# Gate input moved from VectorE to TensorE and ScalarE, and the Newton step of LayerNorm from GpSimd to VectorE

## What is computed

```python
xn = _layernorm(x)                       # (x - mean) / sqrt(var + 1e-5)
s  = scan_forward(xn) + scan_backward(xn)
h  = gelu(xn @ w1[sel] + b1[sel])
g  = silu(xn + 0.3 * ((h @ w2[sel] + b2[sel]) @ Wo + bo))
x  = x + s * g
```

## Time and profile before

| | |
|---|---|
| time, median of 3 runs | 3112.79 us (3112.57 to 3116.84) |
| profiled execution | 3118.2 us, of which its span 3116.4 us |
| VectorE (DVE) busy | 3021.6 us, 97% |
| GpSimd (POOL) busy | 3013.3 us, 97% |
| ScalarE (ACT) busy | 2940.6 us, 94% |
| TensorE (PE) busy, matmuls | 2489.1 us, 80% |
| mean granted clock of TensorE | 0.958 of full |

### The profile page before, as it was taken

How to read it: one execution, slowest core, us unless ns; L and a number is a source line. 1 busy time by engine, 2 the same in 40 slices (tenths; PEclk the granted TensorE clock), 3 DMA queues, 4 the chain that set the end, 5 groups by cost and what they waited for, 6 DMA issues and landing times. The chain is left out here.

```text
span 3116.4 us, 49216 instructions
## 1 busy us (share of the span) xinstructions
PE 2489.1 (80%) x15990; PEld 1970.9 (63%) x15990; DVE 3021.6 (97%) x1995; ACT 2940.6 (94%) x5242; POOL 3013.3 (97%) x1486
## 2 busy tenths in 40 slices
PE   7878878878778888788787788887788887887886
PEld 6666656666656666566666566666666665666665
DVE  3999999999999999999999999999999999999999
ACT  5899999999999999999999999999999999999995
POOL 3899999999999999999999999999999999999997
PEclk9999999999999999999999999999999999999998
DMA  5543334444334444344433444443444433444331
GB/s 174 151 134 116 125 119 130 143 125 119 118 123 141 135 124 123 111 131 143 130 120 119 127 128 140 127 124 111 128 139 134 126 120 114 131 144 130 107 122 55
DMA packets 273364, 394.17 MB, mean 126 GB/s; under 512 B 45003, under 2 KB 119508, under 8 KB 273108
## 3 DMA queue, kind: packets, MB, share of 16 engines
q1 hardware_dynamic: 273108, 391.03, 41.1%
HBM read 348.98 MB, written 25.18 MB: 120 GB/s over the span
## 5 line engine op out<-in xcount | busy, mean ns | idle before, releaser
L480 POOL TENSOR_TENSOR bx<-dx,b_sb 128x1024 f32<-128x1024 f32 x576 | 1362.9, 2388 | 10.2 <-DVE hs L861 9.5
L861 DVE TENSOR_TENSOR_SCAN hs<-decay,bx 128x1024 f32<-128x1024 f32 x576 | 1308.7, 2277 | 8.7 <-ACT decay L682 4.3
L468 POOL TENSOR_TENSOR hc<-hs,c_sb 128x1024 f32<-128x1024 f32 x480 | 1135.7, 2376 | 22.6 <-DVE hs L861 21.1
L1091 PE MATMUL y<-ident,hc 128*128 128x128 f32 x8192 | 1068.6, 277 | 36.0 <-DVE hc L840 36.0
L1091 PEld LDWEIGHTS y<-ident,hc 128*128 128x128 f32 x8192 | 942.0, 143 | 148.5 <-DVE hc L840 106.0
L861 DVE TENSOR_TENSOR_SCAN hs<-decay_sb,decay 128x1024 f32<-128x1024 f32 x448 | 1004.7, 2266 | 11.8 <-issue 10.5
L682 ACT ACTIVATE decay<-delta,rate 128x512 f32<-128x512 f32 x1152 | 745.6, 684 | 38.8 <-DVE hs L861 35.9
L594 ACT ACTIVATE dxb<-dxT,btok 128x256 f32<-128x256 f32 x1792 | 759.2, 503 | 0.3 <-PE decay L1066 0.3
L1066 PE MATMUL decay<-ident,dxb 128*128 128x128 f32 x3584 | 477.2, 276 | 244.9 <-DVE hs L861 212.8
L840 DVE TENSOR_TENSOR hc<-hs,c 128x1024 f32<-128x1024 f32 x544 | 649.6, 1194 | 1.3 <-issue 0.7
L1066 PEld LDWEIGHTS decay<-ident,dxb 128*128 128x128 f32 x3584 | 396.5, 141 | 401.3 <-issue 259.1
(11 more groups left out here) (125 smaller groups left out, 2050.8 us busy)
## 6 DMA issues: line engine op xcount, KB each, us to landing
b_sb<-b_scratch SPq DMA_DIRECT2D x576, 256.0 KB, 3.3
c_sb<-b_scratch SPq DMA_DIRECT2D x480, 256.0 KB, 3.5
xin<-in_L_attn_x_dram SPq DMA_DIRECT2D x32, 512.0 KB, 6.6
w_sb<-in_L_ffn_W_dram SPq DMA_DIRECT2D x32, 512.0 KB, 3.4
w2o_sb<-w2o_scratch SPq DMA_DIRECT2D x32, 512.0 KB
xres<-in_L_attn_x_dram SPq DMA_DIRECT2D x32, 512.0 KB, 5.4
out_dram<-og SPq DMA_DIRECT2D x32, 512.0 KB, 4.3
dbc<-high SPq DMA_DIRECT2D x64, 128.0 KB, 2.3
```

Source lines behind the costliest of these rows:

```text
L468: nc.gpsimd.tensor_tensor(hc[:, s % RING, :, :], hs[:, s % HSLOTS, :, :], c_sb[:, i % CRING, :].unsqueeze(1).broadcast_to([P, DT, T]), ALU ...
L480: nc.gpsimd.tensor_tensor(bx[:, i % RING, :, :], dx[:, g, :, :], b_sb[:, i % BRING, :].unsqueeze(1).broadcast_to([P, DT, T]), ALU.mult).th ...
L861: V.tensor_tensor_scan(hs[:, s % HSLOTS, :, :].rearrange("p k t -> p (k t)")[:, u], factor.rearrange("p k t -> p (k t)")[:, u], data.rearr ...
L1091: ins = M(yps[:, c, k * P:(k + 1) * P], hc[:, s % RING, k, c * P:(c + 1) * P], ident[:, :], start=False, stop=(s == ADDED[-1]), is_transpo ...
```

## The change

The factor 0.3 moves into the stored expert weights and into the bias, so the PSUM bank holds the scaled FFN output; TensorE adds `xn` to it by one more matmul with the identity for each 128 tokens, four a row; and the bank is then only copied, by ScalarE, in the steps in which VectorE read it. The Newton step goes from GpSimd's step 6 to VectorE's step 3, in three instructions; ScalarE's copy of the negated mean is gone. In the setup, VectorE has one more small instruction for the bias, and the first row's Newton step.

```diff
-    MEAN, SCALE, SHIFT, NORM = 0, 1, 6, 6
+    MEAN, SCALE, SHIFT, NORM = 0, 1, 3, 6
-    EPS = 1e-5
+    EPS, FFN_SCALE = 1e-5, 0.3
 # GpSimd
-            def shift_of(row):
-                wait_alone(pool, s_sqr, row * 3 + 3)
-                wait(pool, s_xn, row * C)
-                G.tensor_tensor(nwt[:, :], rsq[:, :], nvar[:, :], ALU.mult).then_inc(s_nwt, 1)
-                G.tensor_scalar(nwt[:, :], nwt[:, :], 1.5, None, ALU.add).then_inc(s_nwt, 1)
-                G.tensor_tensor(rs[:, :], nwt[:, :], rs[:, :], ALU.mult).then_inc(s_nwt, 1)
-                G.tensor_tensor(shift[:, :], nmean[:, :], rs[:, :], ALU.mult).then_inc(s_shift, 1)
 # ScalarE
-                A(nmean[:, :], mv[:, :, 0], ACT.Identity, scale=-1.0).then_inc(s_sqr, 1)
+            def gate_input(row, v):
+                act.wait_ge(s_pf, row * UNITS + 12 + v)
+                if v == 0:
+                    wait(act, s_yg, row)
+                A(zz[:, 2 * v:2 * v + 2, :], fps[:, :].rearrange("p (c d) -> p c d", c=2), ACT.Copy).then_inc(s_zz, 1)
 (in drain)
+                at = GATE if row else GATE_FIRST
+                if s in at:
+                    gate_input(row, at.index(s))
 (in copy_w2o)
-                  ACT.Copy).then_inc(s_w2oc, 1)
+                  ACT.Copy, scale=FFN_SCALE).then_inc(s_w2oc, 1)
 # VectorE
-                wait(dve, s_shift, row)
+            def shift_of(row):
+                dve.wait_ge(s_sqr, row * 2 + 2)
+                wait(dve, s_xn, row * C)
+                V.tensor_tensor(nwt[:, :], rsq[:, :], nvar[:, :], ALU.mult).then_inc(s_nwt, 1)
+                dve.wait_ge(s_nwt, row * 2 + 1)
+                V.scalar_tensor_tensor(rs[:, :], nwt[:, :], 1.5, rs[:, :], ALU.add, ALU.mult).then_inc(s_nwt, 1)
+                dve.wait_ge(s_nwt, row * 2 + 2)
+                V.scalar_tensor_tensor(shift[:, :], mv[:, :, 0], -1.0, rs[:, :], ALU.mult, ALU.mult).then_inc(s_shift, 1)
-            def gate_input(row, v):
-                dve.wait_ge(s_pf, row * UNITS + 12 + v)
-                V.scalar_tensor_tensor(zz[:, 2 * v:2 * v + 2, :], fps[:, :].rearrange("p (c d) -> p c d", c=2), 0.3,
-                                       xn[:, 2 * v:2 * v + 2, :], ALU.mult, ALU.add).then_inc(s_zz, 1)
 (setup, bias)
-            bias_sum = bias_ps[0:NE, 0:D]
+            V.tensor_scalar(bias_sum, bias_ps[0:NE, 0:D], FFN_SCALE, None, ALU.mult).then_inc(s_biass, 1)
+            dve.wait_ge(s_biass, 1)
 # TensorE, ffn_out
-                    ins = M(to, ones3[:, :], bias3[:, :], start=False, stop=True)
+                    M(to, ones3[:, :], bias3[:, :], start=False, stop=False)
+                    ins = M(to, ident[:, :], xn[:, c, :], start=False, stop=True)
```

More of the change, by code:

```diff
@@ L126, in mamba_moe_block @@
         nvar = sb("nvar", [P, C])
-        nmean = sb("nmean", [P, C])
         rsq = sb("rsq", [P, C])
@@ L164, in mamba_moe_block @@
         wo_sb = decay_sb[:, 1, 1, :].rearrange("p (k n) -> p k n", k=DT)
-        bo_row, bias_rest, bias_rest2 = dxb[0:1, 0, 0, :], dxb[0:NE, 0, 1, :], dxb[0:NE, 0, 2, :]
+        bo_row, bias_rest, bias_rest2, bias_sum = dxb[0:1, 0, 0, :], dxb[0:NE, 0, 1, :], dxb[0:NE, 0, 2, :], dxb[0:NE, 0, 3, :]
         w2_in = (w2o_sb, xres)
@@ L202, in mamba_moe_block @@
         s_bias, s_biasc, s_biasst, s_b2T, s_dtz = (sem(n) for n in ("bias_ready", "bias_parts", "bias_stored", "b2T_loaded", "dtw_zeroed"))
+        s_biass = sem("bias_scaled")
         s_proj, s_bstored = sem("projected_copied"), sem("b_stored")
@@ L487, in residual @@
                 nc.gpsimd.tensor_tensor(og[:, :, :], og[:, :, :], xres[:, :, :], ALU.add).then_inc(s_out, 1)
-            def shift_of(row):
-                wait_alone(pool, s_sqr, row * 3 + 3)
-                wait(pool, s_xn, row * C)
-                G = nc.gpsimd
-                G.tensor_tensor(nwt[:, :], rsq[:, :], nvar[:, :], ALU.mult).then_inc(s_nwt, 1)
-                wait_alone(pool, s_nwt, row * 3 + 1)
-                G.tensor_scalar(nwt[:, :], nwt[:, :], 1.5, None, ALU.add).then_inc(s_nwt, 1)
-                pool.wait_ge(s_nwt, row * 3 + 2)
-                G.tensor_tensor(rs[:, :], nwt[:, :], rs[:, :], ALU.mult).then_inc(s_nwt, 1)
-                pool.wait_ge(s_nwt, row * 3 + 3)
-                G.tensor_tensor(shift[:, :], nmean[:, :], rs[:, :], ALU.mult).then_inc(s_shift, 1)
             def front(row, par, s):
-                if s == SHIFT:
-                    shift_of(row)
                 if s in LOG1P:
@@ L512, in front @@
                     cut(row, par, CUT.index(s))
-            shift_of(0)
             log1p(0, 0)
@@ L809, in low_part @@
                 V.tensor_tensor(low[:, :], fps[:, :], high[:, :], ALU.subtract).then_inc(s_lo, 1)
-            def gate_input(row, v):
-                dve.wait_ge(s_pf, row * UNITS + 12 + v)
-                if v == 0:
-                    wait(dve, s_yg, row)
-                V.scalar_tensor_tensor(zz[:, 2 * v:2 * v + 2, :], fps[:, :].rearrange("p (c d) -> p c d", c=2), 0.3,
-                                       xn[:, 2 * v:2 * v + 2, :], ALU.mult, ALU.add).then_inc(s_zz, 1)
             def front(row, par, s):
@@ L820, in front @@
                     mean_variance(row)
+                if s == SHIFT:
+                    shift_of(row)
                 if s == LOW:
                     low_part(row)
-                at = GATE if row else GATE_FIRST
-                if s in at:
-                    gate_input(row, at.index(s))
             def output(row):
@@ L873, in _ @@
             dve.wait_ge(s_xwT, 1)
+            shift_of(0)
             V.tensor_copy(wx[:, :, :], wx_ps[:, 0:2 * P].rearrange("p (k m) -> p k m", k=DT)).then_inc(s_wev, 1)
@@ L918, in _ @@
             dve.wait_ge(s_bias, 1)
-            bias_sum = bias_ps[0:NE, 0:D]
+            V.tensor_scalar(bias_sum, bias_ps[0:NE, 0:D], FFN_SCALE, None, ALU.mult).then_inc(s_biass, 1)
+            dve.wait_ge(s_biass, 1)
             V.tensor_copy(bias_part[:, 0, :], bias_sum).then_inc(s_biasc, 1)
             dve.wait_ge(s_biasc, 1)
-            V.tensor_tensor(bias_rest[:, :], bias_sum, bias_part[:, 0, :], ALU.subtract).then_inc(s_biasc, 1)
+            V.tensor_tensor(bias_rest[:, :], bias_sum[:, :], bias_part[:, 0, :], ALU.subtract).then_inc(s_biasc, 1)
             dve.wait_ge(s_biasc, 2)
```

## The result

The changed kernel takes 3201.93 us (median of 4 runs, 3198.87 to 3203.18). The kernel before, on the same chip, takes 3114.82. The ratio is 1.0277 [1.0259, 1.0295], so the change costs 87 us. The forecast was 3130 (range 3103 to 3148), slower by 17.4 us: the sign was right and the size five times too small, outside the range.

What follows compares the result with a forecast made beforehand. TensorE's gapless stream to broadcast 6 was taken to bound steps 0 to 6, VectorE the rest; 31 rows +18.4 us, first row -1, setup 0: +17.4 on the median 3112.8 gives 3130.2, range 3103 to 3148.

Steps and rivals of the forecast that it cites:

- VectorE, added: Newton step in VectorE's step 3: three dependent 128x4 operations, 0.45 us a row, upper end 0.85.
- TensorE's stream: Four identity matmuls, 1.83 us a row, before the broadcast for state 6's C product; rows grow 0.60 us on average.
- the rival of the late phases: All rows settle like the third or fourth, 95.65 or 95.96 us: +29 to +38 us, 3142 to 3151; chance 0.17.
- the main forecast's four lengths: Rows keep a mix of four clock phases, growing 0.20, 0.70, 0.74 and 0.74 us; 3120 to 3138, chance 0.50.
- VectorE, removed: Two gate inputs leave VectorE, 1.16 us a row, and its waits for the full bank go too.
- GpSimd's four operations: The Newton step leaves GpSimd, 1.13 us of work a row; worth nothing by itself.
- the faster case: TensorE's stream has room, so VectorE sets rows of 93.66 us: -33 us, 3080; chance 0.15.
- ScalarE: Two added copies of a 128x512 bank, 0.96 us a row, costed at nothing because ScalarE idles 3.08 us a row.
- its rival: ScalarE becomes the bound: its step 6 lateness passes on through the factors, up to 30 us more, 3160; chance 0.08.
- VectorE stays the bound: Room in TensorE's stream before broadcast 6 leaves the row to VectorE, -1.06 us a row, 3080; chance 0.15.

Runs made afterwards that it cites:

- the gate half: The changed kernel with the Newton step back on GpSimd as four instructions in step 6: 3140.22 us, ratio 1.007 to the kernel before.
- the run with the early identities: Changed kernel with Newton step back on GpSimd, and the first bank's two identity matmuls put ahead of the wait for GELU: 3107.7 us, ratio 0.997.
- The two fastest kernels: Changed kernel, Newton step on GpSimd, first bank's two identity matmuls ahead of GELU's wait: 3107.7 us; the same with broadcast 6 issued in step 3: 3105.93 us.

## Why the prediction was wrong in its size

**VectorE, added: the step that failed.** The prediction took 0.45 us for the three operations from the setup, with 0.85 as the upper end. The earlier trace rows was a true duration under a condition that I did not look at: GpSimd ran nothing there. In step 3 GpSimd runs one 2.37 us instruction after another, and the step took 3.45 to 4.04 us, 3.0 to 3.6 us too much, or 93 to 111 us in 31 rows. Beside that, VectorE is now the later one in the row, so TensorE's stream, the term that made up the forecast's +17.4, is hidden for the most part: waits for it at C products are down to 1.4 us in the whole run, against 19.9 us in the gate half. The common row adds up from VectorE: 94.37 us of the undisturbed row before, less 1.16 for two gates, plus 4.04 for the step (or 3.45 and a wait of 0.47 before it), plus 0.16 by which the idle time before the scan behind `low` grew (0.36 to 0.52), is 97.41 (or 97.29), against 97.40.

**TensorE's stream: right.** The gate half alone cost 23 us for 17.4 forecast, by the waits named. Its rows lie at one length, 95.57, nearer to the rival of the late phases (95.65 to 95.96) than to the main forecast's four lengths, and its 3140 us lie in that rival's range. The matmul was under-priced: 0.457 us is the mean of four in a row, and each identity matmul stands alone behind a bias matmul, where it took 0.53, which is 2.1 us a row for 1.83. The clock over the first FFN parts stayed at 0.50 in after, as forecast; that matmuls in the idle stretch before them go with a higher clock is seen in the run with the early identities.

**VectorE, removed: right** in size, but it had no worth while the broadcast was late, and in after the wait for GpSimd took back half of it.

**GpSimd's four operations: right** at nothing, for this change, but by a wrong reading. The prediction had VectorE as the bound wherever TensorE was not. GpSimd's own row turned out to be 94.5 us, and the kernel before, with 94.7 us on average, was within 0.3 us of it; the faster case, with rows of 93.66, was not to be had while GpSimd kept its work. The two fastest kernels here are bounded by GpSimd with these operations in it, and no run takes the operations off GpSimd without giving them to VectorE, so what they are worth there is not shown. I asked only what GpSimd's relief was worth, and never what GpSimd's running instructions would do to VectorE's new ones.

**ScalarE: right** at nothing in after and in the gate half, and its rival did not come. With the stream shortened VectorE waits for its factor, but GpSimd has less idle time still.

**The rivals.** That VectorE stays the bound came true by a way that I did not have: through a dearer step, slower, not through room in the stream, faster. No rival had a price above 3160.

## What to carry to other kernels

Before a small operation is moved to another engine, look up its duration where the neighbours are as busy as at the place that it goes to, not in an idle stretch; on VectorE ask which operands it reads from SBUF and what GpSimd runs at that moment. A chain of such operations waits once for each link, so its price is up to one GpSimd instruction a link. Matmuls added to a stream with no gap cost their full time, and in the idle stretch before it they cost nothing here and went with a higher clock behind them: moving two of four turned 1.007 into 0.997. And the engine with the longest waits by name is not the bound; the one without waits is.

## What was not expected of the hardware

- A VectorE operation on one to four elements a partition took between 0.14 and 2.3 us, by its operands' form and by what GpSimd was running. The trace books the wait as busy time, so the table of waits does not show it; VectorE's busy time rose from 3021.6 to 3099.0 us with less to compute, and its share stayed at 97%.
- Twelve 128x1 tensor_scalar with a scalar per partition took 1.71 us beside a running GpSimd, 0.14 us an instruction; three 128x4 took 3.45.
- A matmul of 128x256 f32 at the full clock cost 0.53 us alone between others, and 0.457 on average where four like it follow one another. This goes by its place and not by the identity: its first record took 0.32 us and its second 0.22 (start to start), and where four records with the identity stood in a row at the full clock, they took 0.22 us each, as those of the FFN do.
